# A DLRM tower on one core: one tensor_reduce merges a tile's 24 parts, and GpSimd makes the first layer's products

## The reference, cut to what matters

```python
e = jnp.stack([tbl_f[ids[:, f]] for f in range(40)], axis=1)   # [512, 40, 16]
x = e
for k in (k0, k1, k2):                                         # [128, 40 | 128 | 128, 40]
    x = jnp.einsum('bhd,bmd,ohm->bod', x, e, k)                # [512, 128, 16]
    outputs.append(jnp.sum(x, axis=-1))
h = jnp.concatenate(outputs + [dense_ctx], axis=1)             # [512, 400]
y = relu(relu(h @ W_top1 + b_top1) @ W_top2 + b_top2) @ W_top3
```

## Time and profile before

| | us |
|---|---|
| three runs | 817.72, 821.02, 821.31 |
| median | 821.02 |
| profiled execution, its span | 817.8 |
| PE busy | 690.5 (84%) |
| DVE busy | 668.2 (82%) |
| ACT busy | 523.9 (64%) |
| POOL busy | 499.1 (61%) |

### The profile page before, as it was taken

The page is one execution under the profiler, slowest core; times in us unless marked ns, Lnnn a source line. Parts: engine busy times, 40 slices in busy tenths (PEclk is TensorE's granted clock), DMA queues, the critical chain, the costliest instruction groups (busy, mean ns, idle before and its releaser), DMA issues.

```text
span 817.8 us, 12851 instructions
## 1 busy us (share of the span) xinstructions
PE 690.5 (84%) x2558; PEld 477.1 (58%) x2558; DVE 668.2 (82%) x1542; ACT 523.9 (64%) x1753; POOL 499.1 (61%) x443
## 2 busy tenths in 40 slices
PE   0157988899898979797988898988979797998998
PEld 0126666566565757575655666665657575775384
DVE  2325989898988989898979898989979797989191
ACT  2205676676775767676666776767757676788193
POOL 6304767767667777685867767776767783564000
PEclk9998999999999999999999999999999998998599
DMA  6261111111212121212111111112121211010000
GB/s 187 63 171 61 44 55 53 45 64 38 70 25 76 22 77 25 76 31 69 35 60 46 49 58 45 62 37 70 19 77 22 75 30 64 36 42 26 0 1 1
DMA packets 45543, 43.07 MB, mean 53 GB/s; under 512 B 25615, under 2 KB 28943, under 8 KB 45216
## 3 DMA queue, kind: packets, MB, share of 16 engines
q1 hardware_dynamic: 40352, 41.07, 15.3%
q0 software_dynamic: 5120, 1.32, 2.2%
HBM read 41.06 MB, written 1.97 MB: 53 GB/s over the span
## 4 chain that ended last, share of the span: by engine, by line
DMA 37%; PE 21%; POOL 15%; issue 10%; SPq 7%; DVE 7%; ACT 2%; DVEq 1%; POOLq 0%; ACTq 0%
DMA pairs<-scratch 24%; POOL fold L350 7%; POOL x0g L309 7%; DMA scratch<-x0g 5%; DMA x0g<-in_table,rows_now 4%; DMA scratch<-scratch 4%; PE Y L622 4%; PE Y L624 3%; PE Y L623 3%; DVE chain L534 3%; SPq L268 3%; SPq L278 2%; DVE chain L497 2%; SPq L273 1%; DVE pairs L462 1%
## 5 line engine op out<-in xcount | busy, mean ns | idle before, releaser
L417 ACT ACTIVATE scaled<-Y,xtok 128x128 f32<-128x128 f32 x1536 | 422.7, 380 | 110.8 <-PE Y L624 100.5
L622 PE MATMUL Y<-k1lo,x1hi 128*128 128x512 f32 x640 | 296.5, 463 | 47.8 <-DVE chain L534 46.2
L624 PE MATMUL Y<-k1hi,x1lo 128*128 128x512 f32 x640 | 255.9, 400 | 0.0
L623 PE MATMUL Y<-k1hi,x1hi 128*128 128x512 f32 x640 | 255.4, 399 | 0.0
L534 DVE SCALAR_TENSOR_TENSOR chain<-Y,xtok,chain 128x128 f32<-128x128 f32 x768 | 211.6, 338 | 4.9 <-PE Y L624 4.8
L309 POOL DMA_INDIRECT x0g<-in_table,rows_now x160 | 174.5, 1091 | 42.1 <-issue 36.0
L350 POOL TENSOR_TENSOR fold<-fold,scaled 128x512 f32<-128x512 f32 x128 | 170.8, 1334 | 37.3 <-ACT scaled L417 28.3
L622 PEld LDWEIGHTS Y<-k1lo,x1hi 128*128 128x128 f32 x640 | 122.2, 191 | 118.3 <-DVE chain L534 77.6
L350 POOL TENSOR_TENSOR fold<-scaled 128x512 f32<-128x512 f32 x64 | 91.9, 1437 | 138.3 <-ACT scaled L417 111.1
L462 DVE TENSOR_TENSOR pairs<-pairs,A 120x512 f32<-120x512 f32 x112 | 96.9, 865 | 76.8 <-DMA pairs<-scratch 76.7
L623 PEld LDWEIGHTS Y<-k1hi,x1hi 128*128 128x128 f32 x640 | 122.7, 192 | 38.7 <-issue 14.4
(11 more groups left out here) (77 smaller groups left out, 453.4 us busy)
## 6 DMA issues: line engine op xcount, KB each, us to landing
pairs<-scratch SPq DMA_DIRECT2D x112, 240.0 KB
A<-scratch SPq DMA_DIRECT2D x16, 240.0 KB
k1raw<-in_k SPq DMA_DIRECT2D x1, 2560.0 KB, 10.5
x0g<-in_table,rows_now POOLq DMA_INDIRECT x160
k2s<-in_k SPq DMA_DIRECT2D x1, 2560.0 KB, 17.8
scratch<-x0g SPq DMA_DIRECT2D x64, 20.0 KB
pairs<-in_w SPq DMA_DIRECT2D x3, 256.0 KB
scratch<-scratch SPq DMA_DIRECT2D x16, 40.0 KB
```

The lines of the kernel that those rows point to most:

```text
L417: ins = nc.scalar.activation(scaled[:, rank(c) - 1, i * O:(i + 1) * O], Y[(NCH * tile + c) % YB][:, i * O:(i + 1) * O], ACT.Copy, scale=xt ...
L622: nc.tensor.matmul(y, hi[:, tok], k1lo[:, cols], start=True, stop=False)
L623: nc.tensor.matmul(y, hi[:, tok], k1hi[:, cols], start=False, stop=False)
L624: nc.tensor.matmul(y, lo[:, tok], k1hi[:, cols], start=False, stop=True).then_inc(s_y, 1)
```

## The change

- `scaled`, `fold` and the two `chain` buffers go. In their place are two buffers `sums`, each with six parts of 512 columns, for tiles in turn. ScalarE copies its six scaled chunks into the six parts; part 0 is also what VectorE's running sum adds on to.
- VectorE's four merging adds become one tensor_reduce, which reads the 24 blocks of 128 columns by the view "p (i o) -> p o i" and adds over i: 3072 elements in, 128 out, the step between neighbours in the read 512 bytes. It stands after chunk 3 of the next tile.
- GpSimd's three folding adds go. It makes the first layer's products instead of VectorE, at the same positions, in tile j between diag and that tile's gathers; the seven products of the first group stand ahead of its loop.
- ScalarE's waits for folds and merges at each A chunk become one wait per tile, for the merge of two tiles earlier.
- ph and pl move from 1 and 2 to 4 and 5 positions behind the product, l0 from 6 to 8.

```diff
-FOLDS = 3
-EXTRA = NA - 2 - FOLDS
-MERGE = EXTRA + 3
+PARTS = NA
-XTOK_AT, PROD_AT, PROD_APART, L0_LAG = 14, 6, 3.6, 6
-SPLIT_LAG = {"ph": 1, "pl": 2}
+XTOK_AT, PROD_AT, PROD_APART, L0_LAG = 14, 6, 3.6, 8
+SPLIT_LAG = {"ph": 4, "pl": 5}
-MERGE_AT = (0, 3, 3, 3)
+MERGE_AT = 3
-        scaled = sb("scaled", [P, NA, BANK])
-        fold = [sb(f"fold{i}", [P, BANK]) for i in range(2)]
-        chain = [sb(f"chain{i}", [P, BANK]) for i in range(2)]
+        sums = [sb(f"sums{i}", [P, PARTS * BANK]) for i in range(2)]
+        chain = [t[:, 0:BANK] for t in sums]
...
+            def product(u, slot, c):
+
+                g, par = (u * GPB + slot + 1, (slot + 1) % 2) if slot >= 0 else (0, 0)
+                _, buf, fills = chunk(u, slot, c)
+                pool.wait_ge(s_a3, 16 * (g + 1))
+                pool.wait_ge(s_roll[buf], 16 * (fills + 1))
+                nc.gpsimd.tensor_tensor(pairs[buf][0:PR, :], pairs[buf][0:PR, :], A3[par][0:PR, :],
+                                        ALU.mult).then_inc(s_prod, 1)
...
-                    sums = fold[tile % 2]
-                    pool.wait_ge(s_merge, MERGE * T + 1)
-                    for a in range(2, NA - EXTRA):
-                        pool.wait_ge(s_yA, NA * (T + 1) + a + 1)
-                        if a > 2:
-                            pool.wait_ge(s_fold, FOLDS * (T + 1) + a - 2)
-                        nc.gpsimd.tensor_tensor(sums[:, :], scaled[:, 1, :] if a == 2 else sums[:, :],
-                                                scaled[:, a, :], ALU.add).then_inc(s_fold, 1)
+                    for p in range(j * NCH, (j + 1) * NCH):
+                        for step in steps_at(slot, last, p):
+                            if step[:4] == "prod":
+                                product(u, slot, int(step[4:]))
...
+            def merge(T, par):
+
+                dve.wait_ge(s_chain, STT * (T + 2))
+                dve.wait_ge(s_yA, NA * (T + 2))
+                nc.vector.tensor_reduce(x2[par][:, :], sums[par][:, :].rearrange("p (i o) -> p o i", o=O), AX.X,
+                                        ALU.add).then_inc(s_merge, 1)
```

More of the change, by code:

```diff
@@ L183, in build @@
         w1cs, ctxs = A3[0][0:CTX, :], A3[1][0:CTX, :]
-        z2, w2s = pairs[3], over("fold0", "w2s", [P, H1 // P, H2])
-        h1 = scaled[:, 0:H1 // P, :]
+        z2, w2s = pairs[3], over("sums0", "w2s", [P, H1 // P, H2])
+        h1 = over("sums0", "h1", [P, H1 // P, BANK], skip=4 * H1 // P * H2)
         k2hi, k2lo = k1hi, k1lo
         Ghi = x1hi + pairs_hi[0:2]
-        Glo = x1lo + [pairs_hi[2], over("chain0", "Glo3", [P, B], f32r)]
+        Glo = x1lo + [pairs_hi[2], over("sums1", "Glo3", [P, B], f32r)]
         h2, ys = G[:, 0:2, 0:B], G[0:1, 2, 0:B]
@@ L292, in _ @@
             sp.dma_start(ctxs[:, :], ctxT).then_inc(s_mlp, 16)
-            sp.wait_ge(s_merge, MERGE * (NTILES + 2))
+            sp.wait_ge(s_merge, NTILES + 2)
             sp.dma_start(w2s[:, :, :], w2.rearrange("(c p) n -> p c n", p=P)).then_inc(s_w2, 16)
@@ L323, in _ @@
             pool.wait_ge(s_dones, 2)
-            nc.gpsimd.memset(fold[1][:, :], 0.0).then_inc(s_fold, FOLDS)
             nc.gpsimd.memset(credit[:, 0:1], 0.0).then_inc(s_G, 1)
             nc.gpsimd.memset(credit[:, 1:2], 0.0).then_inc(s_diag, 1)
+            for c in range(NC0):
+                product(0, -1, c)
             def body(u, last):
@@ L406, in body @@
                             if rank(c) == 1:
-                                act.wait_ge(s_chain, STT * T + MB)
-                            elif rank(c) <= NA - EXTRA:
-                                act.wait_ge(s_fold, FOLDS * T + max(rank(c) - 2, 1))
-                            else:
-                                act.wait_ge(s_merge, MERGE * (T + 1) + rank(c) - NA + EXTRA)
+                                act.wait_ge(s_merge, T + 1)
                             if rank(c) == 1:
@@ L415, in body @@
                             for i in range(MB):
-                                m = c * MB + i
+                                m, k = c * MB + i, (rank(c) - 1) * MB + i
                                 ins = nc.scalar.activation(
-                                    scaled[:, rank(c) - 1, i * O:(i + 1) * O],
+                                    sums[tile % 2][:, k * O:(k + 1) * O],
                                     Y[(NCH * tile + c) % YB][:, i * O:(i + 1) * O], ACT.Copy,
@@ L457, in prep @@
                 g, par = (u * GPB + slot + 1, (slot + 1) % 2) if slot >= 0 else (0, 0)
-                if step[:4] == "prod":
-                    _, buf, fills = chunk(u, slot, int(step[4:]))
-                    dve.wait_ge(s_a3, 16 * (g + 1))
-                    dve.wait_ge(s_roll[buf], 16 * (fills + 1))
-                    nc.vector.tensor_tensor(pairs[buf][0:PR, :], pairs[buf][0:PR, :], A3[par][0:PR, :],
-                                            ALU.mult).then_inc(s_prod, 1)
-                elif step[:2] == "pl":
+                if step[:2] == "pl":
                     c = int(step[2:])
@@ L478, in prep @@
                                             ALU.add).then_inc(s_x1free, 1)
[L480 to L501 removed]
+            def merge(T, par):
[3 more added lines that the diff above has]
+                                        ALU.add).then_inc(s_merge, 1)
+            nc.vector.memset(chain[1], 0.0).then_inc(s_chain, STT)
+            nc.vector.memset(sums[1][:, BANK:], 0.0).then_inc(s_szero, 1)
+            nc.vector.memset(credit[:, 4:5], 0.0).then_inc(s_merge, 1)
             dve.wait_ge(s_w0, 32)
@@ L536, in body @@
                                     scalar=xtok[slot % 2][:, j, m:m + 1],
-                                    in1=chain[tile % 2][:, i * O:(i + 1) * O] if n >= MB else scaled[:, 0, i * O:(i + 1) * O],
+                                    in1=chain[tile % 2][:, i * O:(i + 1) * O],
                                     op0=ALU.mult, op1=ALU.add).then_inc(s_chain, 1)
@@ L540, in body @@
                             prep(step, u, slot)
-                        for k in range(MERGE):
-                            if c == MERGE_AT[k]:
-                                merge(T - 1, (tile - 1) % 2, k)
+                        if c == MERGE_AT:
+                            merge(T - 1, (tile - 1) % 2)
             over_groups(dve, body)
-            for k in range(MERGE):
-                merge(NTILES - 1, (NTILES - 1) % 2, k)
-            dve.wait_ge(s_merge, MERGE * (NTILES + 2))
+            merge(NTILES - 1, (NTILES - 1) % 2)
+            dve.wait_ge(s_merge, NTILES + 2)
             for c in range(NCH):
@@ L592, in make_G @@
             def make_G(T, buf):
-                pe.wait_ge(s_merge, MERGE * (T + 3))
+                pe.wait_ge(s_merge, T + 3)
                 pe.wait_ge(s_diag, T + 2)
```

23 lines of the change are left out of this document (1 added, 22 removed).

## The result

The changed kernel takes 918.12 us (median of four runs, 914.88 to 921.86), the kernel before on the same chip 821.16: ratio 1.129, 95% interval 1.122 to 1.137. I had forecast 800, range 764 to 842. The profiled execution took 919.99 us with a span of 918.2, against a span of 817.8 before. Some executions of a kernel fall in a slower state, more than 1.5% above its fastest; every ratio here leaves those out.

The account below looks back on a forecast made before the run. The prediction took the ring of pairs loads and gathers as the bound, with DVE and PE close behind. On the profiled 817.8 us: -20 + 0.6 - 2.6 + 1.2 = -21, 797; the runs' median is 3 higher, so 800, range 764 to 842.

Parts of the forecast that it names:

- The reduce's price: VectorE's merging tensor_reduce of 3072 elements a tile: taken as 3.35 us, with ends of 3.2 and 7.0 us.
- Its sign of being wrong: What the profile would show if the forecast failed: a reduce above 5 us, with PE waiting for it.
- The rule from a price to a time: A slot is the largest of ring, DVE and PE, plus what they cost each other; the reduce costs PE some tenths.
- The Trainium skill's warning: On the reduce's SBUF reads: a 16-byte line wants two hits, so a 512-byte step pays at every element; estimate 6.5 us.
- The rival that came true: The reduce pays for its step: slower from 5.6 us a reduce; at 7.0, a 49.2 us slot and 914 us; chance 0.17.
- The tail: In the last slot, by the rival of the dear reduce, a tile goes from 7.56 to 11.5 us, 16 us more in all.
- The ring: Each slot's cycle of pairs loads, GpSimd's products and gathers, scratch write and A3: its turn shortens from 43.7 to 42.3 us.
- DVE's part: VectorE's work per slot: 39.6 less 13.6 of adds and 4.8 of products, plus 13.4 of reduces, gives 34.6 us.
- GpSimd against the long reduce: Rival: GpSimd's SBUF operations and the reduce exclude each other, 4.7 us a turn, 867 us; chance 0.03.

Follow-up runs that it names:

- side_by_side: The changed kernel with the reduce reading groups of 24 neighbours instead of a 512-byte step (wrong sums): 804.56 us, ratio 0.982.
- price_list: The changed kernel with lone test reduces and adds at growing steps behind its last layer, some beside GpSimd's adds; larger steps cost 1.9 to 2.3 us on 3072 elements.
- merge_first: The changed kernel with its reduce put ahead of VectorE's first chunk of the next tile (MERGE_AT 0 instead of 3): 1011.24 us, ratio 1.241.

## Why the prediction was wrong

- **The reduce's price** is the first step that failed: "I take 3.35, since the nearest row is the same operation at that rate, and its access is the only thing that differs." The access was the price. It measured 5.57, inside the bounds of 3.2 to 7.0. 114 us hang on it, by side_by_side. Its sign of being wrong, "a reduce above 5 us, with PE waiting for it", is what the profile shows.
- **The rule from a price to a time failed as well**: a slot as "max(ring, DVE, PE) plus what they cost each other", with the latter put at "some tenths". Put 5.57 into the prediction's own sum: a turn of 43.5 for 42.3 (17 us), last tiles of 10.05 us for 7.56 (10), a last merge 2.2 dearer: 829 us, an estimate, still inside the range. The other 89 us to 918 are what the engines cost each other.
- **The Trainium skill's warning**, SBUF — State Buffer, section Specifications, was right in kind: two hits in a 16-byte line are enough, and price_list has its cliff exactly between steps of 8 and 16 bytes. My estimate from it of 6.5 us was too high: the second access costs 0.63 to 0.75 ns and not a cycle of 0.96 GHz more (1.04).
- **The rival that came true was mis-sized.** Of it I wrote: "it passes the ring's 42.3 at (42.3 - 21.2)/4 = 5.3 us a reduce, and the old 43.7 at 5.6": at the measured 5.57 that says a turn of 43.5, no slower than before. The turn was 48.6. That 918 lies near its 914 is chance, since that figure went with a reduce of 7.0 us. Shown: the 5.1 us over the sum are waits of VectorE, for TensorE (66.8 us in all) and for ScalarE's first chunk (40.2), they begin between 3.3 and 4.2 us of reduce, and they depend on where the reduce stands (merge_first adds 5.7 a turn at the same busy time). How much of them the lower clock makes is open; TensorE's matmuls for Y took 296.1 + 263.5 + 262.2 us at 0.935 and 290.5 + 254.3 + 254.7 in side_by_side at 0.974, 22 us of the 114, and not all of that is on the path.
- **The tail** came as that rival said, 11.4 us a tile for 11.5, but by luck: 1.3 us of waits more and 1.4 of reduce less.
- **The ring** held: 42.3 was forecast, and 41.8 to 42.6 were measured in the five kernels in which GpSimd made the products and the reduce was cheap. Its terms held too. In this slot of side_by_side, from the landing that product 0 waits for (328.97), product 6 ends at 21.9 us for the 22.7 forecast, and the third gather starts at 24.6 for 25.5:

```profile
328.97 1.30 POOL L315 TENSOR_TENSOR pairs<-pairs,A 120x512 f32<-120x512 f32 x1 [10.07 <-DMA pairs<-scratch]
...
349.61 1.27 POOL L315 TENSOR_TENSOR pairs<-pairs,A 120x512 f32<-120x512 f32 x1 [0.51 <-DMA pairs<-scratch]
...
353.57 0.94 POOL L305 DMA_INDIRECT x0g<-in_table,rows_now  x1 [0.30 <-issue]
```

- **DVE's part** held in its other terms: with the cheap reduce VectorE is busy 39.5 of 50 us, 33.3 a slot, against 34.6.
- **GpSimd against the long reduce**: next to nothing, 0.1 us for the reduce and none for GpSimd's adds (price_list). That agrees with the rule of the Trainium skill cited for that rival, SBUF — State Buffer, Who interferes with whom, by which tensor_reduce never contends on this chip.
- **Not seen**: that the merge by one cheap reduce, the step moved to the writing side, is worth 55 us by itself in the old frame, and that the products on GpSimd, which I counted as the gain, throw 35 to 40 of them away.
